# A four-layer graph network on one core: stage C's first turn as its own stream in another bank, layer 5's moments on VectorE, its last key chunk in another bank, the exchanged adjacency loaded, and a new issue order

## Time and profile before

| | |
|---|---|
| median of 3 runs | 2979.78 us |
| the profiled execution, its own time | 2981.56 us |
| its span, first to last instruction | 2979.8 us, granted TensorE clock 0.997 |
| busy share of the span | PE 99%, PE weight loads 78%, DVE 87%, ACT 79%, POOL 12% |
| DMA over the span | 50.03 MB, mean 17 GB/s |

### The profile page before, as it was taken

The page is one execution under the profiler, slowest core; times in us unless marked ns, Lnnn a source line. Parts: engine busy times, 40 slices in busy tenths (PEclk is TensorE's granted clock), DMA queues, the critical chain, the costliest instruction groups (busy, mean ns, idle before and its releaser), DMA issues.

```text
span 2979.8 us, 89370 instructions
## 1 busy us (share of the span) xinstructions
PE 2937.2 (99%) x35171; PEld 2332.7 (78%) x35171; DVE 2579.1 (87%) x7386; ACT 2362.3 (79%) x6868; POOL 357.8 (12%) x651
## 2 busy tenths in 40 slices
PE   8999999999999999999999999999999999999998
PEld 6777777777777777787777777777777777777777
DVE  5788898898898898898898888888888888988985
ACT  5778878878878878878888888888888788788775
POOL 1111111111111111111111111111111111111110
PEclk9999999999999999999999999999999999999999
DMA  6000000000000000000000000000000000000000
GB/s 213 9 14 11 11 14 11 12 11 14 12 11 14 12 11 14 12 11 14 11 11 14 12 11 12 13 11 12 14 11 12 14 11 12 14 11 12 11 7 7
DMA packets 39406, 50.03 MB, mean 17 GB/s; under 512 B 4688, under 2 KB 38992, under 8 KB 38992
## 3 DMA queue, kind: packets, MB, share of 16 engines
q1 hardware_dynamic: 38992, 44.32, 4.7%
HBM read 31.72 MB, written 12.58 MB: 15 GB/s over the span
## 4 chain that ended last, share of the span: by engine, by line
PE 92%; DVE 3%; ACT 2%; issue 2%; DMA 1%; SPq 0%; POOL 0%; POOLq 0%; ACTq 0%; DVEq 0%
PE bank_a L330 27%; PE bank_c L330 23%; PE bank_b L330 18%; PE bank_c L376 8%; PE bank_b L362 4%; PE bank_b L369 2%; PE bank_c L516 2%; PE bank_b L376 2%; PE bank_c L531 1%; PE bank_a L376 1%; DVE node_b L951 1%; PE bank_c L532 1%; PE bank_c L533 1%; ACT htc_hi L697 1%; DVE row_max L838 1%
## 5 line engine op out<-in xcount | busy, mean ns | idle before, releaser
L717 ACT ACTIVATE prob<-score,neg_head_max 128x128 f32<-128x128 f32 x1536 | 494.1, 391 | 14.8 <-DVE neg_head_max L998 7.0
L330 PE MATMUL bank_c<-htc_hi,w_lo 128*128 128x128 f16 x2304 | 395.8, 219 | 0.0
L330 PE MATMUL bank_c<-htc_lo,w_hi 128*128 128x128 f16 x2304 | 395.8, 219 | 0.0
L330 PE MATMUL bank_c<-htc_hi,w_hi 128*128 128x128 f16 x2304 | 395.8, 219 | 0.0
L330 PE MATMUL bank_a<-w_hi,hta_hi 128*128 128x384 f16 x1152 | 377.1, 328 | 1.9 <-ACT bank_a L596 1.6
L330 PE MATMUL bank_a<-w_lo,hta_hi 128*128 128x384 f16 x1152 | 376.6, 327 | 0.0
L993 DVE SCALAR_TENSOR_TENSOR score<-bank_c,bias 128x384 f32<-128x384 f32 x512 | 282.0, 551 | 76.1 <-PE bank_c L516 72.1
L998 DVE TENSOR_REDUCE neg_head_max<-score 128x3 f32<-128x384 f32 x512 | 281.4, 550 | 6.9
L806 DVE SCALAR_TENSOR_TENSOR pt_lo<-bank_c,pt_hi 128x384 f16<-128x384 f32 x512 | 260.9, 552 | 25.5 <-ACT pt_hi L596 20.5
L330 PE MATMUL bank_a<-w_hi,hta_lo 128*128 128x384 f16 x1152 | 251.5, 328 | 0.0
L376 PE MATMUL bank_c<-ident,prob 128*128 128x128 f32 x1536 | 244.3, 275 | 3.3 <-ACT prob L717 3.3
(11 more groups left out here) (203 smaller groups left out, 9275.6 us busy)
## 6 DMA issues: line engine op xcount, KB each, us to landing
x_in<-x SPq DMA_DIRECT2D x64, 192.0 KB, 2.4
out<-y_out SPq DMA_DIRECT2D x64, 192.0 KB, 1.8
w_stage<-w_t SPq DMA_DIRECT2D x10, 576.0 KB, 5.9
adj_in<-adj SPq DMA_DIRECT2D x64, 64.0 KB, 2.1
score<-w_t SPq DMA_DIRECT2D x5, 576.0 KB, 7.0
prob<-w_t SPq DMA_DIRECT2D x4, 576.0 KB, 7.4
bias_rows<-biases SPq DMA_DIRECT2D x11, 192.0 KB, 5.3
norms<-norm_rows SPq DMA_DIRECT2D x8, 192.0 KB, 6.6
```

Source lines behind the costliest of these rows:

```text
L330: mm = nc.tensor.matmul(out_ap, a, b, start=first and i == 0, stop=last and i == len(pairs_of) - 1, skip_group_check=True)
L717: ex = nc.scalar.activation(prob[:, j, c, :], score[:, j, c, :], ACT.Exp, bias=neg_head_max[:, j, c:c + 1])
```

## The change

1. The adjacency is also given to the kernel with its two node axes exchanged (`adj_turned`). SP loads it into one buffer `adj_t`; POOL multiplies it by the strict lower triangle. The PE transpose, its stream and the DVE step are gone. Stage B's first product now waits for `attn_tb_ready` of the previous graph itself.
2. Layer 4's turn goes to bank c3 and is a stream of its own (`t`), which waits for `pt_lo` of the previous graph's last quad. The wait for `head_out` moves to the scores.
3. Layer 5's moments are made by `bn_stats` and `bn_aggr` on DVE; ACT keeps only the scaling.
4. Layer 5's third key chunk is written to bank c0, and ACT copies the first two chunks as soon as they are there (`k_begun`).
5. `ORDER`, `FIRST`, `SPLITS`, `WARM_FIRST` and `WARM_LAST` are all written anew.

```diff
 ORDER = {
-    "pe": "yyacbwwwwcwwxccaxxcaccccxxxcxayybxxawbwcbyyyyyyyywdbcwwwxxcxxacxxcxccacccbxcxyybyyybay",
+    "pe": "wwwccxcaxxcaccccxxxcxayybxxawcwybyybyyyyywbcwwwxxxxxcacxxacbccxcctcxybyaybyyyyyacbwww",
     (act, dve and pool anew as well)
+            def load_turned(g):
+                if g:
+                    sp.wait_ge(*tri_low_ready.at(g - 1))
+                sp.dma_start(adj_t[:, :], adj_turned[g:g + 1, :, :].rearrange("a p d -> (a p) d")).then_inc(adj_t_loaded[g], 16)
...
             for g in range(2, graphs):
                 load(g)
+                load_turned(g - 1)
                 if g >= 4:
                     store(g - 4)
...
-            def turn_adj(g):
-                pe.wait_ge(*adj_loaded.at(g))
-                if g:
-                    pe.wait_ge(*attn_tb_ready.at(g - 1, 2))
-                nc.tensor.transpose(b1[:, 0:128], adj_in[g % 4][:, :], ident[:, :]).then_inc(adj_t_done[g], 1)
-                yield
...
+            def start_c(g):
+                pe.wait_ge(*node_c_ready.at(g, 1))
+                if g:
+                    pe.wait_ge(*pt_lo_ready.at(g - 1, quad(5, 3)))
+                turned(c3, lambda c: node_c[0][:, c * 128:(c + 1) * 128]).then_inc(tc_done[g], 1)
+                yield
...
-                            mm = columns(bank, m + of, htc_hi, htc_lo, o)
+                            apart = l == 1 and of == 2 and o == CHUNKS - 1
+                            mm = columns(c0 if apart else bank, m + of, htc_hi, htc_lo, o, apart or o == 0)
+                            if l == 1 and of == 2 and o == CHUNKS - 2:
+                                mm.then_inc(k_begun[g], 1)
...
             def middle_c(g):
-                yield from moments("c", g, x2[g % 2], x2_ready.at(g, 2))
                 scale("c", g, node_c[1], x2[g % 2], node_c_ready)
...
-                        yield from outer_norm("c", g)
+                        dve.wait_ge(*x2_ready.at(g, 2))
+                        yield from moments("c", g, 1, x2[g % 2][:, :])
+                        dve.wait_ge(*mean_ready["c"].at(g))
+                        V.tensor_scalar(var_eps["c"][:, :], mean_var["c"][:, 1:2], 1e-5, None, ALU.add)\
+                            .then_inc(var_eps_ready["c"][g], 1)
+                        yield
+                        dve.wait_ge(*root_ready["c"].at(g))
+                        V.scalar_tensor_tensor(shift["c"][:, :], mean_var["c"][:, 0:1], -1.0, rstd["c"][:, :], op0=ALU.mult, op1=ALU.mult)\
+                            .then_inc(shift_ready["c"][g], 1)
+                        yield
...
-            def mask_b(g):
-                dve.wait_ge(*adj_t_done.at(g))
-                V.tensor_tensor(tri_mask[:, 1, :], b1[:, 0:128], upper_lower[:, 1, :], ALU.mult).then_inc(tri_low_ready[g], 1)
-                yield
...
                 P.tensor_tensor(tri_mask[:, 0, :], adj_in[g % 4][:, :], upper_incl[:, :], ALU.mult).then_inc(tri_up_ready[g], 1)
+                yield
+                pool.wait_ge(*adj_t_loaded.at(g))
+                P.tensor_tensor(tri_mask[:, 1, :], adj_t[:, :], upper_lower[:, 1, :], ALU.mult).then_inc(tri_low_ready[g], 1)
                 yield
```

More of the change, by code:

```diff
@@ L41, with gnn_stack_kernel @@
 WARM_FIRST = {
[3 rows of a table removed]
[3 rows of a table added]
 }
 WARM_LAST = {
[5 rows of a table removed]
[5 rows of a table added]
 }
-def gnn_stack_kernel(nc, x, adj, w_t, biases, norm_rows, beta, out, graphs):
+def gnn_stack_kernel(nc, x, adj, adj_turned, w_t, biases, norm_rows, beta, out, graphs):
     f32, f16 = mybir.dt.float32, mybir.dt.float16
@@ L139, in gnn_stack_kernel @@
         shift, total, neg_mean, squares = (
-            {of: sb(f"{n}_{of}", [128, 1]) for of in ("in", "ab", "bc", "c")}
+            {of: sb(f"{n}_{of}", [128, 1]) for of in ("in", "ab", "bc", "c") if of != "c" or n == "shift"}
             for n in ("shift", "total", "neg_mean", "squares"))
         spent = {of: sb(f"spent_{of}", [128, D]) for of in ("in", "ab", "bc")}
-        spent["c"] = node_c[1]
         psum = lambda name: ctx.enter_context(nc.psum_tensor(name, [128, 512], f32))
@@ L318, in _ @@
                 load(g)
+                load_turned(g - 1)
                 if g >= 4:
                     store(g - 4)
+            load_turned(graphs - 1)
             for g in range(max(graphs - 4, 0), graphs):
@@ L346, in rows_rest, with columns @@
                 return product(bank[:, 0:D], [(tl[:, c, :], w_hi[:, m, c, :]) for c in range(CHUNKS)], first=False)
-            def columns(bank, m, th, tl, o):
+            def columns(bank, m, th, tl, o, first):
                 cols = slice(o * 128, (o + 1) * 128)
@@ L354, in columns @@
                             (w_lo[:, m, c, cols], th[:, c, :])]
-                return product(bank[:, cols], ops, first=o == 0)
+                return product(bank[:, cols], ops, first=first)
             def columns_high(bank, m, th, o):
@@ L478, in weight_b @@
                     pe.wait_ge(*htb_hi_ready.at(g, k))
[L479 to L480 removed]
+                    if l == 0 and g:
+                        pe.wait_ge(*attn_tb_ready.at(g - 1, 2))
                     for o in range(CHUNKS):
@@ L504, in chain_c @@
                     layer, k = 4 + l, l + 1
-                    pe.wait_ge(*node_c_ready.at(g, k))
-                    if l == 0 and g:
-                        pe.wait_ge(*head_out_ready.at(g - 1, 2))
-                    turned(c0, lambda c: node_c[l][:, c * 128:(c + 1) * 128]).then_inc(tc_done[g], 1)
-                    yield
+                    if l:
+                        pe.wait_ge(*node_c_ready.at(g, 2))
+                        turned(c0, lambda c: node_c[1][:, c * 128:(c + 1) * 128]).then_inc(tc_done[g], 1)
+                        yield
                     pe.wait_ge(*q_ready.at(g, k))
@@ L512, in chain_c @@
                     pe.wait_ge(*v_lo_ready.at(g, k))
+                    if l == 0 and g:
+                        pe.wait_ge(*head_out_ready.at(g - 1, 2))
                     for c in range(CHUNKS):
@@ L696, in chain_c @@
                     act.wait_ge(*tc_done.at(g, k))
-                    nc.scalar.activation(htc_hi[:, :, :], chunked(c0[:, 0:D]), ACT.Relu).then_inc(htc_hi_ready[g], 1)
+                    nc.scalar.activation(htc_hi[:, :, :], chunked((c3, c0)[l][:, 0:D]), ACT.Relu).then_inc(htc_hi_ready[g], 1)
                     yield
                     act.wait_ge(*v_done.at(g, k))
+                    if l == 0 and g:
+                        act.wait_ge(*pv_done.at(g - 1, 2))
                     copy(v_hi[:, :, 0:HEAD], by_head(c1[:, 0:D])).then_inc(v_hi_ready[g], 1)
@@ L702, in chain_c @@
                     for i, bank, done, ready in ((0, c2, q_done, q_ready), (1, c3, k_done, k_ready)):
-                        act.wait_ge(*done.at(g, k))
+                        if l and i:
+                            act.wait_ge(*k_begun.at(g))
+                        else:
+                            act.wait_ge(*done.at(g, k))
                         if l == 0:
@@ L709, in chain_c @@
                             for c in range(CHUNKS):
+                                if i and c == CHUNKS - 1:
+                                    yield
+                                    act.wait_ge(*k_done.at(g, k))
+                                    bank = c0
                                 ins = nc.scalar.activation(qk[:, c, i, :], bank[:, c * 128:(c + 1) * 128], ACT.Identity,
```

45 lines of the change are left out of this document (24 added, 21 removed), and 24 rows, old and new, of tables (FIRST, WARM_FIRST, WARM_LAST).

## The result

| | before | after |
|---|---|---|
| median of the runs, us | 2979.84 (4 runs) | 2939.23 (2938.72 to 2939.96, 4 runs) |
| span of the profiled execution, us | 2979.8 | 2938.2 |
| period of the steady part, mean of 55 graphs, us | 45.002 | 44.521 |

The ratio is 0.9864, with a 95% interval from 0.9847 to 0.9881: 40.6 us faster, where 30 were forecast. One run of the kernel before, in the set beside the last experiment, took 5941.58 us, twice the others, and is left out of its median.

The account below looks back on a forecast made before the run. PE was taken to set the pace, busy 298.42 of 300 us. Terms of -0.40 us a graph over some 61 graphs (-24.5), with -2.5 at the start and -3 at the end, made -30: 2950 us, range 2930 to 2973.

Parts of the forecast that it names:

- the transpose: On PE: the adjacency's transpose is removed, -0.11 us a graph.
- the v product: On PE behind layer 5's turn: hlR replaces ctx_b as cover for the copy of the turned node, -0.23 us a graph.
- the bias row: On ACT, for hlF: no longer behind the three moments, so hlF's wait goes, -0.16 us a graph.
- The norm chain by DVE: Layer 5's norm: counted from the output product's end, the shift comes at 2.40 us and the chain ends at 3.7.
- x1: On DVE: free of POOL's mask product it takes 0.55 us, a gain of 0.26 by the row, 0.39 by the skill's rule.
- The k copies: ACT's key copies before layer 5's scores: with the last chunk in its own bank, a 0.10 us wait a graph goes.
- Layer 5's turn: On PE: in its earlier place it waits for the norm, +0.10 us a graph, with bounds 0 and 1.09.
- Layer 4's turn: On PE, in bank c3: it waits for the last pt_lo, +0.10 us a graph, with bounds 0 and 0.3.
- The small waits: On PE before PV (0.08 us) and u_b (0.10): only rival C had them go; the forecast counted nothing.
- rival C: No new wait, and small ones before PV and u_b go too: -0.68 us a graph, 2933 us; chance 0.15.
- Start and end: First and last graphs: -2.5 us from an earlier third x (bounds 0 and 4), -3 at the end (1 and 4).
- Rival A: Norm chain on DVE late each graph, layer 5's turn waits the full 1.09 us: +0.49 a graph, 3004 us; chance 0.09.

Follow-up runs that it names:

- the kernel with the norm first: Kernel before with the change's four parts in the old order, but DVE and POOL running layer 5's norm ahead of masks, as in the changed kernel: 3053.22 us.
- the one with the old order: Kernel before with the four parts of the change, each engine's steps kept as near as possible to the order of before: 3018.26 us.
- the experiment with the side product early: The early turn's kernel, with layer 1's first side product ahead of layer 4's scores and its bias row ahead of the key copies: 2960.69 us.
- the early turn: Changed kernel with layer 5's last turn of probabilities ahead of layer 2's matching product on PE, DVE's mask behind the last low part: 2931.97 us.

## Why the prediction was right, and where its terms were off

*What was right.* The kernel is bound by PE, the gain is in gaps of 0.1 to 0.25 us, and the three gaps with a named cause went by the amounts forecast: the transpose (-0.11, shown alone by an experiment), the v product (-0.23 forecast, -0.24 and -0.01 measured), the bias row (-0.16). For the bias row the prediction named one cause, the three moments on ACT. The experiments show a second that it left out: the row also stood behind stage B's exponential, and the new order puts it ahead. With the norm's steps on DVE this second one is what counts (+0.44 and +1.31 in the two kernels with ACT's old order); the two were not taken apart. The norm chain by DVE took what the rows of before gave it, 2.42 against 2.40 up to the shift.

x1 left its contention: 0.26 us faster, as the row had it. The rule of the Trainium skill (SBUF — State Buffer, Who interferes with whom), a full lock-out, would have made it 0.39, the whole overlap. Two more places bear on it, in medians of the steady part: in the kernel with the norm first, stage B's delta lasts 0.50 with a POOL mask beside it for its first 0.35, where it lasts 0.28 or 0.29 alone; in the one with the old order it lasts 0.475 with 0.33 of overlap, and x1 is back at 0.81. The losses are 0.26, 0.21 and 0.19 at overlaps of 0.40, 0.35 and 0.33, each 0.13 to 0.14 less than the overlap. And POOL can be the one that is held: its second mask, which in the old order begins 0.36 behind x1, lasts 0.77 where it lasts 0.45 alone, a loss of 0.31 at an overlap of 0.45. The direction of the rule agrees. Its size would agree too if each operation let go some 0.14 before its shown end; spans on POOL are rough, and no run tells.

*The k copies: -0.10 forecast, 0 measured.* The step that failed is the reading that of the 0.43 from node_b's turn to the scores 0.10 is a wait, because another turn is followed after 0.34. The copies did end 0.10 before the scores, but with the copies 0.49 early the 0.43 stays. The comparison was with another kind of successor: these are products of 32 rows. The experiment with the side product early agrees: there layer 4's scores stand behind a float16 product of 384 columns, 0.55 after the last key copy, and it is followed after 0.256, not 0.163, the same 0.09 more.

*Layer 5's turn: +0.10 forecast, 0 measured.* The chain was right up to the shift; ACT's scaled input ran from 2.69 to 3.38 on the same scale, not from 2.8 to 3.5, and the turn was due at 3.60. This term and the one before are each 0.10 that did not come, with opposite signs; that together they leave the sum as it was is luck.

*Layer 4's turn: +0.10 forecast, +0.17 measured.* The mechanism was the one named, the last pt_lo: the early turn takes 0.14 of it away. The other 0.03 lies within the three transposes of the turn (0.356 from their start to the next step, where 0.328 is usual), stays with the early turn, and is not explained.

*The small waits: nothing forecast, -0.14 measured.* Only rival C had them (0.08 and 0.10). The likely reason, not shown by a run, is that layer 4's turn ahead of the last probability x value product gives DVE and ACT the time. Against this stand the +0.05 of ctx_a and the 0.07 more at layer 4's turn. So the likeliest case's terms sum to -0.40 and the measured ones to -0.48: over 61 graphs 29.3 instead of 24.5. Rival C's sum is wrong by its own terms: 0.60 + 0.08 + 0.10 is 0.78 a graph, not 0.68, which makes 2926, not 2933. The measured 2939 lies between it and the forecast, with one of C's two premises true (the small waits went) and one false (a new wait came).

*Start and end: 5.5 forecast, about 11 in the profiled pair.* This is the larger part of what the forecast lacks. The 2.5 for the start was the third x, and 2.4 is what that wait is worth in the kernel before; in the changed kernel this x is issued at 50.05 instead of 53.79, as the new split places were to bring it, and ACT waits 1.4 for it instead of 4.55. The profiled pair shows 6.4 at the first head_out turn; of the rest, 1 to 2 us may be scatter (the pair's spans differ by 1.0 more than the medians), and some 2 were won while the pipeline fills (node_b's turn of the third graph is 7.0 earlier, that of the first 3.7, and two periods account for 1.0 of the difference). The end brought about 5 instead of 3. Neither was taken apart further.

*Rival A* was given 9%. Its condition, layer 5's turn late behind a norm chain on DVE, did not come about in any kernel with the moments on DVE (0.05 at most). But the price of this change does hang on the queues around that chain: with the moments on DVE in the old order, or with the norm first on DVE and POOL alone, the kernel is slower than before by 38 and 75 us, by the bias row on ACT behind an exponential that waits for DVE. The argument that nothing stands between x2 and the shift but hta_lo held for the turn; that the new order of ACT protects the bias row from the longer DVE queue was not in the prediction.

*Open:* the two ctx_a steps of a graph take 1292 to 1294 and 1373 ns in the four kernels with the old order, and 1346 and 1372 to 1394 in all with the new one; the excess lies behind the first product of each, and no rows say why.

## What to carry to other kernels

Where one engine is 99% busy, cut its timeline into its written steps and compare starts, kernel against kernel: a wait of 0.1 us per round, which the busy share hides (298.42 and 298.76 of 300 us here), is seen there. A gap between two steps is a wait only if its supposed releaser, made earlier, shortens it; compare with the same pair of steps, not with a similar one. In queues that run in order, work that is moved to another engine pushes back what stands behind it there, and then whatever on a third engine is queued behind an instruction that waits for that. Follow this one step further than the moved work: the same four edits gave -41 us with the new order and +38 with the old, mostly because one bias row, ready on its own, stood behind an exponential that was not.

## What the runs showed of the hardware

Between the first of three 128x128 float32 transposes and the first of the products with 32 rows lie 0.42 us, where 0.33 lie between such transposes and float16 products, with the copies that these products read done 0.49 earlier. A float16 product of 384 columns is followed by them after 0.256 instead of 0.163. So the first of them starts 0.09 us later than another product would, whichever of the two stands ahead.

A VectorE operation with two SBUF inputs and a GpSimd mask product that overlap in the profile cost the later one 0.19 to 0.31 us at overlaps of 0.33 to 0.45, each time 0.13 to 0.14 less than the overlap.

The start of this kernel, with its loads of 576 KB, is uncertain by about what edits there are worth: 55.39 to 57.20 us to the same instruction in three kernels, with the same loads and instructions ahead of it.
